# A key-major attention head: all 64 score blocks one way round, the sums above the diagonal by TensorE, the diagonal masks by GpSimd

## The reference, cut to what matters

```
scores = jnp.einsum('bqhd,bkhd->bhqk', Q, K) / math.sqrt(HEAD_DIM)
alpha = jax.nn.softmax(scores, axis=-1)
causal = jnp.tril(jnp.ones((n, n), dtype=bool))
alpha = jnp.where(causal, alpha, jnp.zeros((), dtype=alpha.dtype))
Y = jnp.einsum('bhqk,bkhd->bqhd', alpha, V).reshape(b, n, d)
```

## Time and profile before

| what | us |
|---|---|
| runs of before, median of 3 | 1912.72 (1908.29 to 1913.53) |
| span of the profiled execution | 1938.8 |

### The profile page before, as it was taken

The page is one execution under the profiler, slowest core; times in us unless marked ns, Lnnn a source line. Parts: engine busy times, 40 slices in busy tenths (PEclk is TensorE's granted clock), DMA queues, the critical chain, the costliest instruction groups (busy, mean ns, idle before and its releaser), DMA issues. The chain is left out here.

```text
span 1938.8 us, 31529 instructions
## 1 busy us (share of the span) xinstructions
PE 1658.6 (86%) x10758; PEld 1025.6 (53%) x10759; DVE 1151.0 (59%) x2219; ACT 1268.4 (65%) x1416; POOL 251.4 (13%) x251
## 2 busy tenths in 40 slices
PE   7848999999999999999999742099999999999990
PEld 6623433333333333334333442078988988889880
DVE  6855767768677676676877642045354444554533
ACT  7748999999999999999999710024233333332422
POOL 0000000000000000000000033612111221131111
PEclk9969999999999999999999855589999999999995
DMA  5577010100101101011010121333131412322016
GB/s 174 175 206 234 17 33 16 33 26 23 33 16 33 28 22 33 18 31 30 20 33 16 40 98 50 105 121 89 35 101 16 115 52 67 105 65 63 12 12 183
DMA packets 91081, 124.92 MB, mean 64 GB/s; under 512 B 10240, under 2 KB 76544, under 8 KB 91008
## 3 DMA queue, kind: packets, MB, share of 16 engines
q1 hardware_dynamic: 76416, 106.85, 17.4%
q0 software_dynamic: 14592, 17.06, 4.8%
HBM read 74.78 MB, written 51.18 MB: 65 GB/s over the span
## 5 line engine op out<-in xcount | busy, mean ns | idle before, releaser
L697 ACT ACTIVATE probs<-scores 128x1536 f32<-128x1536 f32 (+1 forms) x384 | 520.6, 1379 | 48.7 <-PE scores L627 43.5
L627 PE MATMUL scores<-aq,ak 98*128 98x512 bf16 (+3 forms) x1280 | 304.1, 352 | 61.5 <-DMA aq<-shift_dram 26.8
L740 DVE TENSOR_REDUCE sums<-expq 128x1 f32<-128x1408 f32 (+6 forms) x448 | 347.3, 827 | 13.8 <-ACT expq L703 13.8
L643 PE MATMUL o_ps<-probs,vh 128*32 128x512 f32 (+3 forms) x2560 | 340.0, 543 | 0.0
L1386 ACT ACTIVATE gate<-up_ps 128x512 f32<-128x512 f32 x128 | 76.5, 598 | 350.8 <-PE up_ps L1278 348.6
L627 PE MATMUL scores<-ak,aq 98*128 98x512 bf16 (+3 forms) x1184 | 264.5, 343 | 17.0 <-ACT probs L697 9.0
L703 ACT ACTIVATE expq<-scores 128x1536 f32<-128x1536 f32 x192 | 274.8, 1449 | 2.0
L627 PEld LDWEIGHTS scores<-aq,ak 98*128 98x128 bf16 x1280 | 96.8, 98 | 235.4 <-ACT probs L697 72.8
L627 PEld LDWEIGHTS scores<-ak,aq 98*128 98x128 bf16 x1184 | 91.2, 98 | 238.5 <-ACT expq L703 94.7
L727 DVE TENSOR_TENSOR hidden<-probs,after 128x384 f32<-128x384 f32 x128 | 70.9, 554 | 243.9 <-ACT probs L697 243.9
L1278 PE MATMUL up_ps<-xeT_hi,wup_hi 128*128 128x512 f32 x512 | 205.7, 402 | 11.4 <-issue 9.9
(11 more groups left out here) (209 smaller groups left out, 2378.8 us busy)
## 6 DMA issues: line engine op xcount, KB each, us to landing
raw<-w_T SPq DMA_DIRECT2D x16, 1024.0 KB, 10.0
split_dram<-parts SPq DMA_DIRECT2D x48, 256.0 KB, 2.9
aq<-split_dram SPq DMA_DIRECT2D x192, 64.0 KB
xe_dram<-blank SPq DMA_DIRECT2D x1, 10560.0 KB, 56.1
raw<-wg_T SPq DMA_DIRECT2D x8, 1024.0 KB, 8.7
xin<-xe_dram SPq DMA_DIRECT2D x8, 792.0 KB, 5.5
ak<-split_dram SPq DMA_DIRECT2D x32, 192.0 KB
xin<-xe_dram SPq DMA_DIRECT2D x8, 528.0 KB, 3.8
```

The source lines that it names most:

```text
L627: last = nc.tensor.matmul(dst[:, at:at + w], still, moving[0:KS, lo:lo + w], start=True, stop=True, skip_group_check=True)
L643: last = nc.tensor.matmul(dst[32 * r:32 * r + 32, BLK - w:BLK], vh[j % 2][:, k, :], probs[:, m % P_RING, at:at + w], start=first, stop=Tru ...
L697: last = nc.scalar.activation(probs[:, m % P_RING, 0:w], src[:, 0:w], ACT.Exp, scale=HD ** -0.5)
L740: last = nc.vector.tensor_reduce(sums[:, j % 2, col:col + 1], expq[:, n % X_RING, at:at + w], AX.X, ALU.add)
```

## The change

All 64 blocks of a head (16 groups of 128 keys by 4 groups of 512 queries) are now key-major and full width. `BLOCKS` lists them: for each group g of queries first the four blocks on the diagonal, then the other twelve. Three blocks make a tile, so 21 tiles of 1,536 columns and one of 512; again 32,768 columns. ACT exponentiates all of them into `probs`. `ORDER`, `expq`, `sums`, `den`, DVE's sums and DVE's masks are gone.

The products now come in 16 units of four blocks per head. A block below the diagonal goes through `vh`, one above it through `only_sum`, which gives only its column sum. Unit 4g is the diagonal one (`diagonal`): of each of its four blocks the part above the square goes through `only_sum` or the part below it through `vh`, and the squares go whole through `only_sum`. POOL copies each 128 x 128 square into `seen` with the part above the diagonal set to zero (`affine_select`), and `masked` adds its product with 16 columns of `vh`, ahead of unit 4g+2. Unit u stands behind the fill of the tile that holds its last block, plus 2; a group's turn one tile behind its last unit. So 16 of the 22 fills have a unit behind them, in runs of three with a fill without one between.

ACT has one wait more in some tiles: before it overwrites a tile of `probs` that held diagonal blocks, the masks of those must be done (`mask_done`). The constants `upto` and `after` and their set-up are gone.

```diff
-DVE_ORDER = ((0, "mask", 0), (1, "take", 3), (0, "sum", 0), ...
+BLOCKS = [(g, k) for g in range(NG) for k in list(range(4 * g, 4 * g + 4)) + [k for k in range(NT) if k // 4 != g]]
+UNIT_AT = {}
+for u in range(NU):
+    UNIT_AT.setdefault(tile_of(4 * u + 3) + S_RING, []).append(u)
+TURN_AT = {tile_of(16 * g + 15) + S_RING + 1: g for g in range(NG)}
+DVE_ORDER = ((1, "take", 3), (1, "gather", 3), (1, "final", 0), (0, "take", 0), (0, "gather", 0), (0, "take", 1), (0, "gather", 1),
+             (0, "take", 2), (0, "gather", 2))
...
+                def mask(i, j, g):
+                    pool.wait_ge(exp_done, i * (2 * NS) + (j * NS + tile_of(16 * g + 3) + 1 + S_RING))
+                    pool.wait_ge(pv_done, i * (2 * NU) + (j * NU + NU + 4 * g - 8 + 3))
+                    pool.sem_inc(masking, 1)
+                    for r in range(4):
+                        nc.gpsimd.affine_select(out=seen[:, g % 2, r, :], in_=slot(j, 16 * g + r)(P * r, P * (r + 1)), compare_op=ALU.is_ge, fill=0.0,
+                                                base=0, pattern=[[1, P]], channel_multiplier=-1).then_inc(mask_done, 1)
...
+                def diagonal(j, g):
+                    dst = o_ps[g % O_RING]
+                    for r in range(4):
+                        lo = P * (r + 1)
+                        if r < 3:
+                            nc.tensor.matmul(dst[32 * r:32 * r + 32, lo:BLK], vh[j][:, 4 * g + r, :], slot(j, 16 * g + r)(lo, BLK),
+                                             start=True, stop=True, skip_group_check=True)
+                        else:
+                            last = nc.tensor.matmul(dst[32 * r:32 * r + 32, 0:lo], only_sum[:], slot(j, 16 * g + r)(0, lo),
+                                                    start=True, stop=True, skip_group_check=True)
+                    for r in range(3):
+                        lo = P * (r + 1)
+                        last = nc.tensor.matmul(dst[32 * r:32 * r + 32, 0:lo], only_sum[:], slot(j, 16 * g + r)(0, lo),
+                                                start=False, stop=True, skip_group_check=True)
+                    return last
+                def masked(j, g):
+                    for r in range(4):
+                        nc.tensor.matmul(o_ps[g % O_RING][32 * r:32 * r + HD, P * r:P * (r + 1)], vh[j][:, 4 * g + r, 0:HD], seen[:, g % 2, r, :],
+                                         start=False, stop=True, skip_group_check=True)
+                def products(i, j, u):
+                    g = u // 4
+                    if u % 4 == 0:
+                        pe.wait_ge(out_read, i * (2 * NG) + (j * NG + g + 1))
+                        last = diagonal(j % 2, g)
...
+                        if u % 4 == 2:
+                            pe.wait_ge(mask_done, i * (8 * NG) + (j * (4 * NG) + 4 * g + 4))
+                            masked(j % 2, g)
+                        for n in range(4 * u, 4 * u + 4):
+                            k = BLOCKS[n][1]
+                            r = k % 4
+                            last = nc.tensor.matmul(o_ps[g % O_RING][32 * r:32 * r + 32, :], vh[j % 2][:, k, :] if k < 4 * g else only_sum[:],
+                                                    slot(j % 2, n)(0, BLK), start=False, stop=True, skip_group_check=True)
```

More of the change, by code:

```diff
@@ L35 @@
 BOUND_MAX = 30.0
-KSPAN = 3 * BLK
 NG = N // BLK
[L43 to L72, removed]
@@ L75 @@
[L75 to L89, removed]
@@ L90 @@
[L90 to L121, removed]
@@ L124 @@
[L124 to L132, removed]
+SPAN = 3
@@ new lines, with tile_of, width_of, last_unit @@
+KSPAN = SPAN * BLK
+BLOCKS = [(g, k) for g in range(NG) for k in list(range(4 * g, 4 * g + 4)) + [k for k in range(NT) if k // 4 != g]]
+NBK = len(BLOCKS)
+NS = -(-NBK // SPAN)
+NU = NBK // 4
+S_RING, P_RING, O_RING = 2, 4, 2
+assert 2 * NS % P_RING == 0 and NS % S_RING == 0
+def tile_of(block):
+    return block // SPAN
+def width_of(t):
+    return (min(SPAN * t + SPAN, NBK) - SPAN * t) * BLK
+def last_unit(t):
+    return min(SPAN * t + SPAN - 1, NBK - 1) // 4
+def masks_in(t):
+    return max([4 * (n // NT) + n % NT + 1 for n in range(SPAN * t, min(SPAN * t + SPAN, NBK)) if n % NT < 4], default=0)
@@ L304, in _ @@
                 pe.wait_ge(w_split, 3)
[L305 removed]
+                pe.wait_ge(consts_ready, 8)
                 with pe.Fori(0, NB // 2) as i:
@@ L532, in program @@
             probs = sb(st, "probs", [P, P_RING, KSPAN])
[L533 removed]
             vh = [sb(st, f"vh{j}", [P, NT, 32]) for j in range(2)]
             only_sum = sb(st, "only_sum", [P, 32])
[L536 to L537 removed]
+            seen = sb(st, "seen", [P, 2, 4, P])
             o_sb = sb(st, "o_sb", [P, O_RING, BLK])
             num = sb(st, "num", [P, NT, HD + 1])
[L540 to L541 removed]
             inv = sb(st, "inv", [P, NT])
@@ new lines, in fill @@
+                    for n in range(SPAN * t, min(SPAN * t + SPAN, NBK)):
+                        (g, k), at = BLOCKS[n], n % SPAN * BLK
+                        last = nc.tensor.matmul(scores[t % S_RING][:, at:at + BLK], ak[j][0:KS, k * P:(k + 1) * P],
+                                                aq[j][0:KS, g * BLK:(g + 1) * BLK], start=True, stop=True, skip_group_check=True)
+                    last.then_inc(scores_ready, 1)
+                def diagonal(j, g):
[13 more added lines that the diff above has]
+                    return last
@@ L661, in turn, with behind @@
                     last.then_inc(out_turned, 1)
+                def behind(i, j, t, older, newer):
+                    for back in (1, 0):
+                        if (older and back) or (newer and not back):
+                            for u in UNIT_AT.get(t + back * NS, ()):
+                                products(i, j - back, u)
+                            if t + back * NS in TURN_AT:
+                                turn(i, j - back, TURN_AT[t + back * NS])
                 def head(i, j, older):
-                    pe.wait_ge(a_loaded[j], i * (16 * (A_DMAS + 1)) + 16 * (A_DMAS + 1))
+                    pe.wait_ge(a_loaded[j], i * (16 * LOADS) + 16 * LOADS)
                     pe.wait_ge(vh_ready, i * 2 + (j + 1))
@@ L668, in head @@
                         fill(i, j, t)
-                        for back, work, which in AFTER[t]:
-                            if older or not back:
-                                (products if work == "unit" else turn)(i, j - back, which)
+                        behind(i, j, t, older, True)
                 head(0, 0, False)
@@ L677, in _ @@
                         head(i, j, True)
+                pe.wait_ge(exp_done, pairs * (2 * NS) + S_RING)
                 for t in range(NS):
-                    for back, work, which in AFTER[t]:
-                        if back:
-                            (products if work == "unit" else turn)(pairs, -back, which)
+                    behind(pairs, 0, t, True, False)
             @block.scalar
```

160 lines of the change are left out of this document (44 added, 116 removed).

## The result

| | before | after |
|---|---|---|
| median of the runs, us | 1911.55 (1908.29 to 1913.53, 4 runs) | 2059.16 (2058.34 to 2061.55, 4 runs) |
| span of the profiled execution, us | 1938.8 | 2058.1 |
| one head, us | 30.19 | 34.95 |

The ratio is 1.0764, with a 95% interval of 1.0742 to 1.0786. The change is slower by 147.6 us. The forecast was 2054 us, 2020 to 2110.

The account below looks back on a forecast made before the run. ACT bounds the kernel before, with PE close behind; PE becomes the bound. Its fills, units, turns and waits sum to 34.84 us per head against 30.19, +141.5 us over the kernel: 1912.7 + 141.5 = 2054 us, range 2020 to 2110.

Parts of the forecast that it names:

- The sum per head: PE's work per head: fills 15.53, units 16.85, turns 2.00, turn waits 0.46, together 34.84 us; chance 0.82.
- turn waits: PE in tiles 2 and 18: the turn waits 0.23 us each for the copied unit result, 0.46 us per head.
- the place named as closest: PE's fill, unit, fill without a unit: 2.41 us against 2.39 through ACT, so just no wait.
- The bound: TensorE replaces ACT as the bound, with 6.4 us per head more than ACT needs; ACT busy about 84%.
- From heads to time: 32 heads of 34.84 us, third head's DMA wait absorbed: last unit ends 1237.9, before 1096.0; +141.5 us overall.
- Taking the 26 us above the median as unchanged: Profiled span lay 26 us above the median; +141.5 us applied to both: span 2080, time 2054 us.
- The lower end of the sum's own range: Per head on PE: turns don't wait and products of `seen` lie in the handover, 33.9 us, 2024 us.
- The rival of the diagonal unit in program order: Diagonal unit on PE: no matmul starts ahead of an earlier one, 0.42 us more per unit, 2108 us; chance 0.08.
- The rival of late masks: POOL's masks stall ACT and PE from 1.15 us a square; at 1.5 us about 2190 us; chance 0.03.
- The rival of no loss: PE's handovers (0.15 and 0.09) vanish once work is queued: 30.5 us per head, 1915 us; chance 0.04.

## Why the prediction was right

- **The sum per head.** 34.84 forecast, 34.94 measured. The starts on PE over one head (652.43 to 687.37) break it up: turn waits 0.22 + 0.18 = 0.40 (forecast 0.46), PE waiting for ACT 0.05 + 0.10 + 0.04 + 0.09 = 0.28 (forecast "just none"), and all fills, units and turns 34.26 (forecast 34.38). That the sum is off by only 0.10 is in part luck: 0.28 us of waits and 0.18 less elsewhere cancel. All four small waits stand where only two fills and a plain unit, 2.41 us, lie between a fill and the second one after it. That is the place named as closest. The prediction counted some ten such places, and four lose time; a fill's start lies up to 2.49 us ahead of the second fill after it, so the way through ACT is up to 0.1 us longer than the 2.39 of the sum.
- **The bound.** TensorE became it: 149.5 of 150 us busy, ACT 86% (forecast 84%).
- **From heads to time.** The load of `wr` moved from 1100.42 to 1245.96, by 145.5 us; the forecast was 141.5. 32 x 0.10 = 3.2 of the 4.0 are the step above, 0.4 is a later first fill (120.13 against 119.69). The third head has no DMA wait, as forecast. The medians differ by 147.6.
- **Taking the 26 us above the median as unchanged** was the one step that failed in its form: the stall was not in the changed kernel's execution, so its span is 2058.1, not the 2080 forecast for it. The forecast time was right because the 26 us were subtracted again.
- **The lower end of the sum's own range**, 33.9 us and 2024, does not come out of its terms: 34.84 - 0.46 - 0.84 = 33.54 us, which is 2012. Nothing came near it.
- **The turn waits** were seen where they were forecast and in their size, but not as a cost that a better place would save; the later turns showed it.
- **The rival of the diagonal unit in program order** (2108 us) is out. The program issues L585 three times, L588, then L592 three times; in the rows above the first L592 starts at 677.81, ahead of an L585 at 677.90, and the unit takes 1.00 us, not 1.42. The rule of the Trainium skill (TensorE: Matmul & The Clock Gate, What overlaps and what doesn't), that matmuls start and end strictly in program order, does not hold in these rows.
- **The rival of late masks** is out at 0.29 us a square, and three times that is hidden too. Its threshold was about right, its price was too low: it left out the fourth square.
- **The rival of no loss**, that the handover vanishes, is out: with PE busy without a gap a unit still takes 1.00 us, and one of 208 columns 0.49, which is 0.15 over its columns.

## What to carry to other kernels

A sum of start-to-start distances on the engine that becomes the bound forecast this time within 0.3%; the busy durations of the rows would not have. The runs here fit the reading that two engines coupled through two buffers go at the pace of the slower one in each stretch: work was worth more when it was taken off evenly (3.74 us a head against 2.24 for about the same 6). And a wait on the bounding engine is a cost only if nothing else would have held it there. Before a float32 product is put on an engine that is already 95% busy, price it in bfloat16: the bfloat16 version was the only key-major one that beat the kernel before, and the kernel before gains from bfloat16 too (0.9940).

## What was not expected of the hardware

- A 32-column float32 unit whose strips run beside one another costs its longest strip plus 0.15 us: 1.00 us at 512 columns, 0.49 at 208.
- The granted clock fell to 1.2 GHz inside 8 of the 32 heads when the kernel before got cheaper products, and each of these heads gave back 1.7 us. It had not fallen there in the slower float32 version. It fell the same way in 11 heads of the kernel without upper products and in most heads with six masks, and it held from 150 to 1,235 us in the changed kernel. A wait of PE alone does not decide it: the one of 0.91 us stands in heads where the clock holds too, and with five masks PE waits up to 1.2 us and it holds. The cause stays open.
- A stall of about 28 us in the routing comes and goes between executions. It is in the profiled executions of before, of before in bfloat16 (28.8) and of the kernel with five masks, and in none of the nine others; on the chip of the last two the kernel before took 1941.07 us in the median instead of 1911. No engine of the core ends it in the trace, and its cause stays open.
